# FP4 rounding of the down weight, taken from the NF4 loop to the second and third column block of the FP4 gate and up product

## The reference, cut to what matters

```python
def nvfp4_qdq(x, select_num):
    D = x.shape[-1]
    s = jnp.maximum(jnp.max(jnp.abs(x)) / (448.0 * 6.0), 1e-12)
    xb = (x / s).reshape(x.shape[:-1] + (D // BLOCK, BLOCK))
    sb = jnp.clip(jnp.max(jnp.abs(xb), axis=-1, keepdims=True) / 6.0, 1e-12, 448.0)
    a = xb / sb
    q = jnp.sign(a) * FP4_LEVELS[jnp.digitize(jnp.abs(a), FP4_BOUNDS)]
    dq = (q * sb).reshape(x.shape) * s
    keep = jnp.arange(D) >= D - select_num
    return jnp.where(keep, x, dq)
...
xq = nvfp4_qdq(x2[:, up_reorder_index], SEL_UP)
wg = nvfp4_qdq(w_gate[:, up_reorder_index], SEL_UP)
wu = nvfp4_qdq(w_up[:, up_reorder_index], SEL_UP)
h = jax.nn.silu(xq @ wg.T) * (xq @ wu.T)
hq = nvfp4_qdq(h[:, down_reorder_index], SEL_DOWN)
wd = nvfp4_qdq(w_down[:, down_reorder_index], SEL_DOWN)
out = hq @ wd.T * mlp_output_scale
```

## Time and profile before

| | us |
|---|---|
| median of 3 runs | 804.11 |
| lowest and highest | 802.10 and 804.88 |
| the profiled execution | 802.01 |
| its span in the trace | 800.7 |

### The profile page before, as it was taken

The page is one execution under the profiler, slowest core; times in us unless marked ns, Lnnn a source line. Parts: engine busy times, 40 slices in busy tenths (PEclk is TensorE's granted clock), DMA queues, the critical chain, the costliest instruction groups (busy, mean ns, idle before and its releaser), DMA issues.

```text
span 800.7 us, 10753 instructions
## 1 busy us (share of the span) xinstructions
PE 718.0 (90%) x3832; PEld 535.9 (67%) x3832; DVE 554.1 (69%) x1065; ACT 448.2 (56%) x579; POOL 218.6 (27%) x208
## 2 busy tenths in 40 slices
PE   2898866999999998989988999988899999989998
PEld 1665422656677665667666777766677789967886
DVE  6979977563597767869798876667554434577883
ACT  3778787565877767877875722354432221244452
POOL 1023000004374653646577454211401000000000
PEclk9999966999999999989998999999999999979999
DMA  9636689867476677657765310201301011200001
GB/s 349 184 137 213 188 271 280 263 203 228 129 227 194 204 229 231 205 189 241 228 211 189 97 41 27 76 19 48 105 15 50 23 40 29 61 1 14 27 27 40
DMA packets 55541, 110.79 MB, mean 138 GB/s; under 512 B 9904, under 2 KB 20560, under 8 KB 55232
## 3 DMA queue, kind: packets, MB, share of 16 engines
q1 hardware_dynamic: 42912, 80.28, 31.4%
q10 hardware_dynamic: 8192, 15.73, 5.9%
q0 software_dynamic: 4384, 14.09, 5.9%
HBM read 92.19 MB, written 17.89 MB: 137 GB/s over the span
## 4 chain that ended last, share of the span: by engine, by line
PE 56%; DVE 19%; ACT 9%; issue 9%; DMA 4%; POOL 1%; ACTq 1%; SPq 1%; DVEq 0%; POOLq 0%
PE bank L1245 15%; PE bank L1247 14%; PE bank L1246 14%; ACT hot L1667 2%; PE bank L1359 2%; DVE x L2034 2%; DMA wide_buf<-in_down_flat 2%; ACT c L1627 2%; DVE bank L1949 2%; PE bank L1557 1%; DVE hot L1923 1%; PE bank L1372 1%; PE bank L1401 1%; DVE stats L1844 1%; ACT w_h L1675 1%
## 5 line engine op out<-in xcount | busy, mean ns | idle before, releaser
L1667 ACT ACTIVATE hot<-rep,levels 128x2048 f16<-128x2048 f16 x94 | 192.9, 2093 | 16.7 <-ACT c L1627 10.6
L1245 PE MATMUL bank<-zt_h,w_h 128*128 128x512 f32 (+1 forms) x232 | 94.8, 409 | 2.2 <-DVE zt_l L2022 2.0
L1247 PE MATMUL bank<-zt_h,w_l 128*128 128x512 f32 (+1 forms) x232 | 92.6, 399 | 0.0
L1246 PE MATMUL bank<-zt_l,w_h 128*128 128x512 f32 (+1 forms) x232 | 92.4, 398 | 0.0
L1245 PE MATMUL bank<-w_h,xq_h 128*128 128x512 f32 (+1 forms) x192 | 73.8, 384 | 2.2 <-ACT xq_l L1759 1.9
L1246 PE MATMUL bank<-w_l,xq_h 128*128 128x512 f32 (+1 forms) x192 | 71.6, 373 | 0.0
L1247 PE MATMUL bank<-w_h,xq_l 128*128 128x512 f32 (+1 forms) x192 | 71.5, 372 | 0.0
L1359 PE MATMUL bank<-hot,diag 128*32 128x512 f16 x856 | 64.7, 421 | 2.5 <-ACT hot L1667 2.5
L2178 POOL TENSOR_TENSOR q_a<-q_a,q_m 128x384 f32<-128x384 f32 (+3 forms) x34 | 35.7, 1051 | 85.1 <-DVE q_m L1808 85.0
L2240 POOL TENSOR_TENSOR at_l<-ztok,at_h 128x512 fp32r<-128x512 f32 x28 | 37.5, 1341 | 56.0 <-ACT at_h L1699 55.9
L1245 PEld LDWEIGHTS bank<-zt_h,w_h 128*128 128x128 f32 (+1 forms) x232 | 44.6, 192 | 12.0 <-DVE zt_l L2022 2.4
(11 more groups left out here) (221 smaller groups left out, 1703.1 us busy)
## 6 DMA issues: line engine op xcount, KB each, us to landing
rep<-codes SPq DMA_DIRECT2D x56, 512.0 KB, 4.7
codes<-c SPq DMA_DIRECT2D x28, 256.0 KB, 5.1
raw<-in_codes_gu_t ACTq DMA_DIRECT2D x14, 512.0 KB, 6.1
sc<-in_scales_gu_t SPq DMA_DIRECT2D x56, 128.0 KB, 3.2
raw<-in_codes_attn_t ACTq DMA_DIRECT2D x7, 512.0 KB, 3.8
raw<-in_codes_down_t ACTq DMA_DIRECT2D x7, 512.0 KB, 7.1
sc<-in_scales_down_t SPq DMA_DIRECT2D x28, 128.0 KB, 3.5
wide_buf<-in_gate_flat SPq DMA_DIRECT2D x5, 512.0 KB, 4.7
```

The lines of the kernel that those rows point to most:

```text
L1245: PE.matmul(psum, lh, rh, start=first, stop=False, **kw)
L1246: PE.matmul(psum, lh, rl, start=False, stop=False, **kw)
L1247: return PE.matmul(psum, ll, rh, start=False, stop=last, **kw)
L1667: S.activation(hots[plan.slot[hot_ring(t), (t, m)]][:], codes_in_place(t), ACT.Relu, bias=levels[:, at:at + 1], scale=levels[:, at + 1:at ...
```

## The change: what it does, and the diff

The twelve roundings of the down weight leave the side generator `fp4_weights`, which keeps gate and up (22 roundings) and runs at FP4_RATE = 0.55. A new generator `down_weights` runs beside `hidden(1)` and `hidden(2)` at DOWN_RATE = 2.0 yields for each token tile, so that one rounding falls to each tile: roundings (0,0) to (1,3) beside the eight tiles of block 1, (2,0) to (2,3) beside the first four of block 2. A rounding (c, o) covers column block c (512, 512 or 352 columns) of output channels o.

The rows to be rounded are now gathered into parts of `zt_raw` and of `hid`, which at that time are free or become so. The gather for block 0 waits for steps of the rounding of x; the one for block 1 waits for row turn (2,1) on PE, and the one for block 2 for `wturn` (0,3) and for row turn (2,5), the last one. Rate of the row turns: one for each tile of block 1 (before, 1.25). Each load of a rounded piece waits for its store. The loads take the four buffers in another order (DOWN_BUFS), and two of these are free only after `wturn` (1,3).

```diff
-FP4_RATE = 0.8
+DOWN_BUFS = (3, 2, 0, 1)
+DOWN_RATE = 2.0
+FP4_RATE = 0.55
...
-STREAM = [(name, c) for name in ("gate", "up", "down") for c in range(len(CHUNKS))]
+STREAM = [(name, c) for name in ("gate", "up") for c in range(len(CHUNKS))]
...
-    third = fetch_pair(2)
-    weave(hidden(1), Side(third, 1.25))
+    def down_gather(c):
+        p.add("gather", "down", c)
+        p.sends(f"gather_down{c}", ("gather", "down", c), len(row_tiles(c)))
+
+    def down_weights():
+        items = [("down", c, o) for c in range(len(CHUNKS)) for o in range(KD)]
+
+        def turn(i):
+            if i < len(items):
+                p.add("wturn", *items[i])
+                turn4(("w", *items[i]), ("dve", "wread", *items[i]))
+
+        down_gather(1)
+        turn(0)
+        yield
+        for i, key in enumerate(items):
+            turn(i + 1)
+            if key[2] == KD - 1 and key[1] == 0:
+                down_gather(2)
+            wround(key)
+            yield
+            if i:
+                wfinish(items[i - 1])
+            yield
+        wfinish(items[-1])
+
+    down_gather(0)
+    third, rounded = fetch_pair(2), down_weights()
+    next(third)
+    weave(hidden(1), Side(third, 1.0), Side(rounded, DOWN_RATE))
     p.add("hpart", 1)
     p.add("rec", "h", 1, None)
     drain(third)
-    p.inherit("down", [("late", 8, i) for i in range(4)])
-    weave(hidden(2), Side(itertools.chain.from_iterable(map(down_rows, range(3))), 1.75))
+    p.inherit("down", [("late", 8, i) for i in DOWN_BUFS])
+    p.rings["down"][2:] = [(("pe", "wturn", "down", 1, KD - 1),)] * 2
+    weave(hidden(2), Side(rounded, DOWN_RATE), Side(itertools.chain.from_iterable(map(down_rows, range(3))), 1.75))
...
+                if c == 1 and n >= 4:
+                    act.wait_ge(*done("pe", "wturn", "down", 0, KD - 1))
                 S.activation(hid[:, n, f0:f0 + w], main4(("g", c, n))[:, 0:w], ACT.Silu).then_inc(sem("hfin_act"), 1)
...
+                if name == "down":
+                    pool.wait_ge(*done("pe", "low_a", 1))
+                    if c == 0:
+                        pool.wait_ge(*done("dve", "round", "x", 4, 0))
+                        pool.wait_ge(*done("act", "kept", "x", 4, 0))
+                    elif c == 1:
+                        pool.wait_ge(*done("pe", "rowturn", 1, len(plan.rows[1]) - 1))
+                        pool.wait_ge(*done("pe", "rowturn", 2, 1))
+                    else:
+                        pool.wait_ge(*done("pe", "wturn", "down", 0, KD - 1))
+                        pool.wait_ge(*done("pe", "rowturn", 2, len(plan.rows[2]) - 1))
...
+                sp.wait_ge(*landed(("wstored", "down", c, ch)))
+                SP.dma_start(down_buf(c, ch)[:, 0:w],
                              scr["down"][ch * P:(ch + 1) * P, f0:f0 + w]).then_inc(dma_sem(("down", c, ch)), 16)
```

More of the change, by code:

```diff
@@ L496, in maxima, with wround, wfinish @@
         yield
+    def wround(key):
+        p.add("wround", *key)
+        p.note("wread", *key)
+        p.take("q_tmp", 2, ("w", *key), ("pool", "wfinish", *key))
+        p.take("q_out", 2, ("w", *key), ("dma", ("wstored", *key)))
+    def wfinish(key):
+        p.add("wfinish", *key)
+        p.sends(f"q_out{p.slot['q_out', ('w', *key)]}", ("wstored", *key))
     def fp4_weights():
@@ L502, in gather @@
                 p.add("gather", name, c)
[L503 to L507, removed]
+                p.sends(f"gather_in{n % 2}", ("gather", name, c), KD)
         gather(0)
@@ L1257, in phase_ends @@
         queue.wait_ge(*done("pe", "dn_mm", NG - 1, NT - 1))
-        queue.wait_ge(*done("pe", "wturn", "down", len(CHUNKS) - 1, KD - 1))
+        last_name, last_c = STREAM[-1]
+        queue.wait_ge(*done("pe", "wturn", last_name, last_c, OUTER[last_name][last_c] - 1))
         weights_end(queue)
         queue.wait_ge(*done("act", "cast", len(jobs) - 1))
[L1261 to L1264, removed]
+        for name, c in STREAM:
+            for o in range(OUTER[name][c]):
+                queue.wait_ge(*landed(("wstored", name, c, o)))
     def fp4_source(item):
@@ L1308, in wround_size, with down_rows_at @@
         return min(P, fw - o * P), D, D - KEPT
+    def down_rows_at(c):
+        own = [zt_raw[:, part, 3 * D:4 * D] for part in range(2)]
+        if c == 0:
+            return *own, hid[:, 4, D:2 * D], hid[:, 6, D:2 * D]
+        if c == 1:
+            return *(zt_raw[:, 1, i * D:(i + 1) * D] for i in (6, 7)), *(zt_raw[:, 0, i * D:(i + 1) * D] for i in (4, 5))
+        return *own, zt_raw[:, 0, 7 * D:8 * D]
     def zt_vacant(ln, n):
@@ L1323, in down_vacant @@
         return [(sem("hmm_pe"), 2 * plan.nth["hmm", 1, NT - 1])] if c < 2 else [
-            done("pe", "rowturn", 2, len(plan.rows[2]) - 1)]
+            done("pe", "rowturn", 2, len(plan.rows[2]) - 1), done("pe", "wturn", "down", 2, KD - 1)]
     def down_weights(c, part, lo, hi):
@@ L1384, in pe_program @@
                 f0, fw = CHUNKS[c]
-                tiles, width = (row_tiles(c), D) if name == "down" else ([(t, P) for t in range(KD)], fw)
-                orow, w = min(P, width - o * P), 0
-                for t, rows in tiles:
-                    col = t * width + o * P
-                    last = PE.transpose(bank[0:orow, w:w + rows], wide[0:rows, col:col + orow],
-                                        ident[0:rows, 0:rows])
-                    w += rows
+                if name == "down":
+                    for t, rows in row_tiles(c):
+                        last = PE.transpose(bank[:, t * P:t * P + rows], down_rows_at(c)[t][0:rows, tok(o)],
+                                            ident[0:rows, 0:rows])
+                else:
+                    wide, orow = wide_bufs[STREAM.index((name, c)) % 2], min(P, fw - o * P)
+                    for t in range(KD):
+                        last = PE.transpose(bank[0:orow, tok(t)], wide[:, t * fw + o * P:t * fw + o * P + orow], ident)
                 last.then_inc(sem("wturn_pe"), 1)
@@ L1596, in pe_program @@
                 c, ch = key
-                bank, src, w = turn(("down", c, ch)), late_bufs[plan.slot["down", ("down", c, ch)]], CHUNKS[c][1]
+                bank, src, w = turn(("down", c, ch)), down_buf(c, ch), CHUNKS[c][1]
                 pe.wait_ge(*landed(("down", c, ch)))
@@ L2218, in pool_program @@
                     pool.wait_ge(*done("dve", "gm_max", *GM_ALL[-1]))
[L2219 to L2226 removed]
+                for t in range(KD):
+                    gather(wide[:, t * fw:(t + 1) * fw], a[f"{name}_t{c}"], up_idx[:, t:t + 1], ("gather", *key))
             elif kind == "wround":
```

40 lines of the change are left out of this document (20 added, 20 removed).

## The result

The changed kernel takes 811.25 us (median of 4 runs, 810.62 to 811.88) against 803.23 for the kernel before in the same comparison (802.10 to 804.88): a ratio of 1.0101 with a 95% interval of 1.0079 to 1.0123. It is slower, by 8.0 us where 4.9 were forecast, and 2.2 us above the forecast time of 809.

A forecast was written before the change was run, and what follows sets the result against it. PE was taken to bound the kernel (busy 718.0 of 800.7 us), DVE next. From 802.0 us, -15 in the loop and +21 in blocks 1 and 2 gave 808, as a median 809; likeliest case 803 to 815, overall range 792 to 820.

The forecast's parts named there:

- A: Likeliest case: loop -15 us, blocks 1 and 2 +21, so 809 us, in itself 803 to 815; chance 0.48.
- The loop, forecast -15: NF4 loop without twelve roundings: transposes 4, waits 7 and clock 4 give 15 us back, bounds 4 and 31.5.
- The wait at the scaling: NF4 loop: PE's wait for DVE's scaling falls from 16.8 to 9.9 us, so 7 go.
- Blocks 1 and 2, forecast +21: Hidden product: the stage pays transposes 4.8, waits 14.4 and clock 2, together 21 us; bounds 9.4 and 28.
- `hup` of tile 5: Block 1: POOL's queued gathers delay rounding (0,3), then DVE's (1,1); PE waits 2.8 us in tile 7.
- The first load: Block 2: load (0,0) stands behind the store of (1,2) in SP's queue; PE waits 4.4 us.
- there DVE and POOL still catch up: Block 1: its gather holds POOL until row turn (2,1), but within PE's slack of two tiles.
- The clock is the term: Blocks 1 and 2: three gaps over 2 us may each bring a half-clock stretch; 2 us in all.
- B: Rival: blocks 1 and 2 hide their roundings and cost only 9.4 us, so 798 us, faster; chance 0.20.
- C: Rival: the NF4 loop gives nearly all, -31 with blocks +21, so 794 us, faster; chance 0.12.
- D: Rival: the loop gives only -6 while the blocks cost 21 to 24, so 820 us, slower; chance 0.14.
- E: Rival: loop -20 and blocks +20, no change, 804 us; chance 0.06.

The follow-up runs named there:

- e5: The changed kernel with FP4_RATE put back from 0.55 to 0.8, the rate before the change; 817.94 us, ratio 1.0141 to the kernel before.
- e3: The changed kernel with the POOL gathers of block 2 two roundings later and those of block 1 one rounding later; 799.95 us, ratio 0.9939 to the kernel before.
- e2: The changed kernel with only the three POOL gathers of block 2 moved two roundings later; 804.17 us, ratio 0.9985 to the kernel before.
- e7: The kernel of e3 with the row turns ahead of the turn and the rounding in block 2; 795.06 us, ratio 0.9853 to the kernel before.
- e4: The changed kernel with the first four down loads asked for in the last steps of block 1's roundings; 810.34 us, ratio 1.0058 to the kernel before.
- e8: The edits of e3 and e4 together on the changed kernel; 799.86 us, ratio 0.9920 to the kernel before.
- e10: The kernel of e7 timed again in more rounds; 793.90 us, ratio 0.9890 to the kernel before.
- e9: The kernel of e7 with FP4_RATE 0.5 in place of 0.55; 792.93 us, ratio 0.9884 to the kernel before.
- e1: The changed kernel without any rounding of the down weight, which is loaded as given; 785.53 us, ratio 0.9737 to the kernel before.

## Why the prediction was right, point by point

The likeliest case, A, came true: 811 in 803 to 815, by its two terms of opposite sign and by the waits that it named. How near it came is luck in part. Both terms were too small, the loop's by 5 us and the blocks' by 3.5, and these errors nearly cancel: -15 + 21 = +6 was forecast for them, +4.3 measured. The profiled execution then lost another 4.9 us ahead of the loop, where nothing was to move.

The medians differ by 8.0 us, 3.7 more than these two stretches. In the ten experiments the difference of the medians is within 1.7 us of what the two stretches give. Whether the changed program itself lengthens the stages ahead of the loop or only these executions did is open: the first `gu_mul` comes at 199.9 to 204.7 us in the eleven traces of kernels with the change, and at 198.9 in the only one without it.

**The loop, forecast -15, measured -20.2.** The wait at the scaling went from 16.8 to 9.4 us, where 9.9 was worked out by counting roundings between scalings. That is the step that carried best. Between the two marks PE's idle time fell by 7.8 us, from 22.5 to 14.7. The clock was under-sized: summed over windows of 5 us, the full-speed work lost to it fell from 10.2 to 3.4 us, so 6.8 and not 4. That leaves 5.6 us for the transposes, of which the 44 fewer PE instructions (1543 against 1499) are the count: 4.8 had been worked out and 4 taken, since part of them was to fall into PE's waits, and the measured times don't show that. e5 adds what the prediction didn't separate: 7.5 of the 20.2 us are the spacing of the roundings that stay.

**Blocks 1 and 2, forecast +21, measured +24.5.** The transposes, 4.8, are in line with the 44 more PE instructions (496 against 452) and with what waits and clock leave of the 24.5. The waits were forecast at 14.4 and measured at 13.9, but not one for one:

- `hup` of tile 5: 2.8 forecast, 4.7 measured. POOL's finish came at T + 7.6 by the forecast; row turn (2,5) ended at 647.3 and the finish at 655.4, 8.1 later. Then rounding (1,1) took 5.1 us (655.49 to 660.58), not 3.9: three operations on 128 x 32 elements took 0.45, 0.91 and 1.10 us while POOL's own, at 655.35, 656.71 and 658.05, ran beside them. This is the slow kind of rounding which the rule of the Trainium skill, "SBUF — State Buffer", section "Who interferes with whom", would have for all: the two long ones end as a POOL operation does (657.10 + 0.91 = 658.01 against 656.71 + 1.26 = 657.97, and 659.14 against 658.05 + 1.06 = 659.11). From the opening reduction to the next `hup`, the eight roundings of block 1 took 3.3, 3.3, 5.1, 3.9, 3.3, 5.1, 3.9 and 4.4 us, 4.0 in the mean; the three short ones ran where POOL was idle. I had taken 3.9 for each and kept that rule out of the sum, which is near in the mean; at (1,1) the 1.2 us reached PE.
- `hup` of tile 6: 0.7 forecast, none seen. The first load: 4.4 forecast, 3.3 measured. Load (0,1): 0.5, none seen.
- The bank that rounding (2,1) reads: 2.8 forecast, 3.45 measured. The later two banks: 0.8 and 0.9 forecast, one of 0.84 seen. Load (1,3): 1.5 forecast, 0.46 measured.
- Not forecast: 1.1 us of PE for a bank that DVE has still to read in a rounding of block 0 (L2050), from the gather of block 1 holding POOL. That "there DVE and POOL still catch up" was wrong, and e3 against e2 shows the price, 4 us: with that gather moved, PE has no such wait, and DVE is less late afterwards.

**The clock is the term that was mis-sized most**: 2 forecast. Summed over windows of 5 us, 5.1 us of full-speed work were lost (0.05 x 107.5 = 5.4 by the rounded mean), of which the windows behind the three long gaps show 0.66, 0.71 and 0.68. I had argued that after a gap DVE or a load sets the pace, so that a slow PE costs nothing. PE was busy for 5.00 of 5 us in two of these three windows, so it did cost. 4.8 + 13.9 + 5.1 = 23.8 of the 24.5.

**What the experiments say of the causes.** The two named queues were not equals. POOL's queue was the largest cause: moving the gathers gave 10.5 of the stage's 24.5 us. The order of the row turns gave 3.3 more (e3 to e7, 97.0 to 93.7). SP's loads were a follower: asking for them earlier gave nothing twice (e4, e8), since the same engine, DVE, stood behind both waits. The forecast had given each its own price and summed them. The sum was near since they lie one after the other on one chain of lateness; e4 and e8 show that the price of the loads would not have gone by itself.

**The rivals.** B, 798 us, is near what e3 measures (799.95), though by other terms (-20.2 and +14.0 for B's -15 and +9.4): the prediction's reason against it, the order of POOL's queue, is what had to be changed. It named 9.4 us as the lower bound of the stage's cost; e7 is at 10.7. C and D are out by the loop's 20.2, which lies between the 8 and the 22 us named for them, though nearer to the upper one. E had the loop right, -20, but not the blocks (+20, measured +24.5), and its "no change" is outside the interval.

What stays open: how much of the 3.7 us of waits left in e7 the shared way to memory costs. Its small operations on DVE are stretched in the trace (the rescaling of the reciprocals, 128 x 32 elements, takes 701 ns on average over the eight roundings of block 1, and 180 ns in the first, where POOL is idle), but no run here took POOL's work away without the rounding.

## What to carry to other kernels

Before an instruction with a late condition is put into an in-order queue, ask what stands behind it and who waits for that: here three gathers that stood two roundings too early cost the stage 6 us, and four others, one rounding too early, 4. When side work is moved to a stage without idle time on its critical engine, its price is the added instructions, the waits, and the slow clock behind each long wait; the last was as large as the first. A wait for a load that vanishes when the load is asked for earlier, without a gain in time, had another lateness behind it. And a forecast by terms is to be checked term by term between marks within the stages: the end of the loop moved by the very 15 us of the forecast, and the loop by 20.

## What the runs showed of the hardware that was not expected

- A gap of 3.3 to 4.7 us in an otherwise busy PE was followed each time by a stretch at the half clock that took about 1.6 us of full-speed work (windows of 0.66, 0.71 and 0.68 above). Near 2.6 us it is not certain: the gap of 2.60 in e10 was followed by two windows of 2.5 us at 0.67 and 0.65, that of 2.58 at the same place in e9 by none below 1.00. The gap of 1.10 in the changed kernel, at 634 us, brought none either. In the loop two waits of PE close together (1.59 and 2.09 us, up to 308.0 and 310.5) lie in three windows at 0.93, 0.50 and 0.89, 3.4 us.
- The attention stage, which no edit touches, loses between 15.4 and 22.1 us of full-speed work to the clock ahead of 200 us, from one execution to the next: 22.1 in the changed kernel, 20.5 before, 15.4 in e1, e3 and e10. The mean clock of the first 200 us, in the changed kernel and in e10:

```profile
0.00:200.00 200.00, 151.07 (x901) 97.76 (x902) 144.63 (x258) 134.03 (x160) 24.99 (x27) 0.89 0.71 231
```

```profile
0.00:200.00 200.00, 149.30 (x910) 97.16 (x911) 144.03 (x258) 134.28 (x161) 24.75 (x27) 0.92 0.71 232
```

  So two traces are best compared from mark to mark within a stage, and not by their spans or by the time at which a stage ends. Whether the runs that stray by 3 us do so for this reason is likely and not shown: the timed runs have no windows.
